# Distance attention: one add-and-maximum instruction per head and key tile in place of an add and a separate maximum per chunk

## The reference

```
q, k, v = ... .reshape(B, S, 16, 8)
scores = einsum('bqhd,bkhd->bhqk', q, k) / sqrt(8)
pos_emb = dist_emb[MAX_POS - 1 + distance]
scores = scores + einsum('bqhd,qkd->bhqk', q, pos_emb)
scores = scores + einsum('bkhd,qkd->bhqk', k, pos_emb)
probs = softmax(scores, axis=-1)
ctx = einsum('bhqk,bkhd->bqhd', probs, v)
```

## Time and profile before

| | us |
|---|---|
| median of 3 runs | 3696.86 |
| lowest and highest | 3695.2, 3696.99 |
| the profiled execution | 3662.5 |
| its span | 3660.7 |
| busy in the span: PE, DVE | 3164.8, 3031.9 |
| busy in the span: ACT, POOL | 2661.5, 996.2 |
| the distance attention in it | about 2230 to 3315 |

### The profile page before, as it was taken

The page is one execution under the profiler, slowest core; times in us unless marked ns, Lnnn a source line. Parts: engine busy times, 40 slices in busy tenths (PEclk is TensorE's granted clock), DMA queues, the critical chain, the costliest instruction groups (busy, mean ns, idle before and its releaser), DMA issues. The chain is left out here.

```text
span 3660.7 us, 70796 instructions
## 1 busy us (share of the span) xinstructions
PE 3164.8 (86%) x26908; PEld 2015.8 (55%) x26908; DVE 3031.9 (83%) x4286; ACT 2661.5 (73%) x2303; POOL 996.2 (27%) x1009
## 2 busy tenths in 40 slices
PE   4799999999999999999889756998999999998990
PEld 2233333333333333333568736888888888886890
DVE  8899999999999999999665576788788788786662
ACT  3799999999999999999444334776776776764430
POOL 2111111111111111111215355344343353330436
PEclk9899999999999999999879967999999999998995
DMA  5788898899888998898422254122122122102122
GB/s 157 293 334 338 338 341 332 341 342 342 333 339 338 341 341 332 340 345 337 179 76 56 60 192 77 30 41 41 29 38 43 28 37 43 28 11 76 46 62 68
DMA packets 311190, 683.32 MB, mean 187 GB/s; under 512 B 155281, under 2 KB 228466, under 8 KB 310418
## 3 DMA queue, kind: packets, MB, share of 16 engines
q1 hardware_dynamic: 302226, 661.80, 52.2%
q0 software_dynamic: 8704, 17.84, 2.1%
HBM read 90.66 MB, written 52.10 MB: 39 GB/s over the span
## 5 line engine op out<-in xcount | busy, mean ns | idle before, releaser
L1021 PE MATMUL psA<-wave,diag 128*128 128x512 f32 x2560 | 1171.2, 604 | 80.8 <-DVE score L1190 64.2
L1090 ACT ACTIVATE wave<-wave 128x2048 f32<-128x2048 int32 x640 | 1187.0, 1907 | 46.0 <-DMA wave<-score 39.5
L1021 PEld LDWEIGHTS psA<-wave,diag 128*128 128x128 f32 x2560 | 467.3, 190 | 687.9 <-issue 533.8
L953 POOL TENSOR_TENSOR diag<-ident,par 128x128 f32<-128x128 f32 x384 | 142.9, 401 | 1289.9 <-PE psA L1021 1289.4
L1143 DVE TENSOR_SCALAR score<-s,par 128x2048 int32<-128x2048 int32 x384 | 480.2, 1277 | 6.3 <-DMA wave<-score 6.1
L2248 POOL COPY kb<-ks 48x1024 bf16<-48x1024 bf16 x160 | 321.1, 2007 | 566.8 <-PE psR L2308 380.6
L1190 DVE SCALAR_TENSOR_TENSOR score<-wave,par,score 128x1024 f32<-128x1024 f32 x384 | 469.5, 1276 | 0.0
L1190 DVE SCALAR_TENSOR_TENSOR score<-wave,par,psA 128x1024 f32<-128x1024 f32 x256 | 315.6, 1273 | 47.7 <-PE psA L1021 47.4
L2398 ACT ACTIVATE W<-psR 128x1024 f32<-128x1024 f32 x256 | 249.5, 1023 | 133.3 <-PE psR L2333 133.2
L2389 ACT COPY r<-psR 128x1024 f32<-128x1024 f32 x256 | 248.6, 1020 | 102.4 <-PE psR L2308 102.4
L2435 DVE TENSOR_REDUCE mx<-S 128x8 f32<-128x1024 f32 x256 | 305.4, 1214 | 2.2
(11 more groups left out here) (287 smaller groups left out, 4795.1 us busy)
## 6 DMA issues: line engine op xcount, KB each, us to landing
wave<-score SPq DMA_DIRECT2D x384, 1023.9 KB, 6.3
wave<-s SPq DMA_DIRECT2D x128, 1023.9 KB, 4.8
ks<-kb_parts SPq DMA_DIRECT2D x56, 384.0 KB, 6.0
qs<-qb_parts SPq DMA_DIRECT2D x32, 384.0 KB, 6.3
ys<-f_ys SPq DMA_DIRECT2D x36, 256.0 KB, 2.5
wave_out<-og SPq DMA_DIRECT2D x33, 256.0 KB, 7.2
o<-wave_out SPq DMA_DIRECT2D x8, 1024.0 KB, 9.5
qp<-qa_parts SPq DMA_DIRECT2D x32, 192.0 KB, 7.1
```

Source lines behind the costliest of these rows:

```text
L1021: mm = pe.matmul(psA[:, kt, :], diag[:, h % 2, f, :], wave[:, h % 2, f, kt * L:(kt + 1) * L], start=(f == 0), stop=(f == PE_F - 1 or (h in ...
L1090: act.activation(wave[:, h % 2, f, :], angle[:, h % 2, f, :], ACT.Sin, scale=float(TWO_PI / 2.0 ** 32)).then_inc(sine, 1)
```

## The change

The add of a chunk, one instruction over 8 heads, becomes 8 instructions of one head each. Each adds the two parts, writes 128 columns of S, and leaves the maximum over them, taken with the lowest float32, in its place of `mx`. The last of the eight raises `dve_took`. The maximum steps of the first three units of a block and the semaphore `maxed` are gone; in the fourth unit the step keeps only the reduction from `mx` to `m`. The order on VectorE is otherwise as before, without the steps that are gone. TensorE, ScalarE, GpSimd and SyncE keep their instructions and order.

```diff
@@ -2034,6 +2034,7 @@
+    LOWEST = float(np.finfo(np.float32).min)
@@ -2081,13 +2082,12 @@
     def dve_head(u, q):
-        a, x = chunks("add", u), chunks("max", u)
+        a = chunks("add", u)
         ctx = [("ctx", q, 0)] if q is not None else []
-        return [a[0]] + ctx + [x[0], a[1], x[1], a[2], x[2], a[3], x[3]]
+        return [a[0]] + ctx + a[1:]
 
     def dve_mixed(u, ctx):
-        a, x = chunks("add", u), chunks("max", u)
-        return ctx + [a[0], a[1], x[0], x[1], a[2], a[3], x[2], x[3]]
+        return ctx + chunks("add", u)
@@ -2175,7 +2175,6 @@
-        maxed = sem(c, "maxed")
@@ -2425,17 +2424,18 @@
-                dve.tensor_tensor(part, psR[:, n % RING, :, :].rearrange("p a (h n) -> p (a h) n", n=P), second,
-                                  ALU.add).then_inc(dve_took, 1)
+                both = psR[:, n % RING, :, :].rearrange("p a (h n) -> p (a h) n", n=P)
+                for j in range(HB):
+                    h = k * HB + j
+                    ins = dve.tensor_tensor_reduce(out=part[:, j, :], in0=both[:, j, :], in1=second[:, j, :],
+                                                   scale=1.0, scalar=LOWEST, op0=ALU.add, op1=ALU.max,
+                                                   accum_out=mx[:, h, kt:kt + 1])
+                ins.then_inc(dve_took, 1)
 
             def maximum(u, k):
-                q, kt = u // QT, tile_of(u)
                 hs = slice(k * HB, (k + 1) * HB)
                 dve.wait_ge(dve_took, by_dve["c", u, k])
-                dve.tensor_reduce(mx[:, hs, kt], S[:, hs, kt * P:(kt + 1) * P], AX.X, ALU.max).then_inc(maxed, 1)
-                if u % QT == QT - 1:
-                    dve.wait_ge(maxed, 4 * u + k + 1)
-                    dve.tensor_reduce(m[:, hs], mx[:, hs, :], AX.X, ALU.max).then_inc(m_ready, 1)
+                dve.tensor_reduce(m[:, hs], mx[:, hs, :], AX.X, ALU.max).then_inc(m_ready, 1)
```

## The result

The changed kernel takes 3731.74 us, median of four runs (3731.34 to 3742.69), against 3696.93 for the kernel before: ratio 1.0097 over all runs (the two medians alone give 1.0094), 95% interval 1.0077 to 1.0117. It is slower, by 35 us. The direction was as forecast, and the time lies at the lower end of the range, but the forecast was +143 us, four times too much. Of the cases named, it came out near rival 1, for which 3730 had been worked out.

The account below looks back on a forecast made before the run. TensorE, nearly full, waits for PSUM slots that VectorE's adds free. Mixed units 5.56, first 2.05 and fourth 1.33 make 8.94 us a block, 143 over 16; with the median of 3696.86, forecast 3840 us, range 3725 to 4010.

Parts of the forecast that it names:

- rival 1: VectorE's additions: leaving the maximum is free, t = 0.20, +0.35 a mixed half, 3730 us in all; chance 0.15.
- What bounds the stage: Distance attention: TensorE nearly full, waiting for VectorE's adds to free PSUM slots; the maxima almost free, 0.10 us showing.
- One sign given for it: Waits in the distance attention: VectorE's wait for PE, 199.7 us before, was to become smaller.
- I take 0.27: VectorE's add-and-maximum: 0.27 us a step, the addition's 0.20 plus one more tiny instruction at 0.07.
- t: Time from one 128-column add's start to the next, 0.20 to 0.44 us; a slot is held for 8t and about 0.08.
- +2.05 and +1.33: Microseconds added per block in its first and its fourth unit, as later slots delay PE's chunks.
- the lower end: Lower limit of t: 0.20 us, the step of plain 128-column additions, if the maximum costs nothing.
- 33 and 143 us: Whole-stage losses over 16 blocks of queries: 33 us with t = 0.20, 143 us with t = 0.27.
- the copies would give some back: Where POOL's copies meet the subtractions, later subtractions could give back up to 8 us in four blocks.
- rival 3: TensorE idles in every half of the distance attention and its clock falls, windows under 0.9; chance 0.18.
- Rival 2: VectorE's instructions each wait for the one before or stream slower: t 0.33 to 0.44, 4167 us at 0.44; chance 0.20.
- Rival 4: Mixed halves: slot free earlier only under t = 0.155; at 0.134 a half gains 0.17, 3686 us; chance 0.02.

Follow-up runs that it names:

- E4: Changed kernel with the same instructions, each slot handed back to TensorE in halves: 3666.59 us, ratio 1.0028 to the kernel before.
- E3: Kernel before with wide adds but without its 256 maxima, the maximum left out of the softmax: 3648.54 us, ratio 0.9971.
- E1: Kernel before with each add cut into 8 plain additions, old separate maxima kept: 3712.77 against 3658.30 us, ratio 1.0148.
- E2: Changed kernel with plain additions that leave no maximum, the maximum left out of the softmax: 3685.30 us, ratio 1.0077 to the kernel before.
- E5: Changed kernel with slots handed over in halves both ways between TensorE and VectorE: 3692.35 us, ratio 0.9960 to the kernel before.
- E6: Kernel before with halves both ways, two adds of 512 columns and the old maxima: 3690.88 us, ratio 0.9956.
- E8: Halves both ways, wide adds and separate maxima in three units, new instruction only in the fourth: 3639.98 against 3658.24 us, ratio 0.9946.

## Why the prediction was right and wrong

- **What bounds the stage: right.** PE and VectorE meet in the slot; a longer hold is paid, the maxima were nearly free. E4 shows the first, E3 the second (10 us for 311), and E1 shows the loss without the new instruction. One sign given for it was wrong: VectorE's wait for PE was to be smaller, and it grew from 199.7 to 386.4 us, as its work had shrunk.
- **The step that failed is "I take 0.27".** The term was t, from one addition to the next: 0.20 to 0.44 by the rows, 0.27 chosen by charging one more small instruction in the queue, 0.07. No row of the kernel before shows an instruction of this kind, so the 0.27 was my estimate. The second instruction is there, but it starts when the next addition does, and costs 0.0085 a step against the earlier trace rows (0.211 for 0.2025), or 0.013 against the plain additions of E2 (0.198). At 16 steps in half a mixed unit, 0.06 too much each is 0.94 us a half. With the right t the first add and the second are spaced by PE again, not by VectorE, and of the +2.05 and +1.33 forecast for the first unit and the fourth, +0.78 and +0.14 are left.
- **The argument for the choice was the weak part.** Rows of small independent instructions were taken for the price of one that follows its own main instruction. The four small instructions of the earlier trace rows take a step of 0.07 (four in 0.36 us); the write of the maximum adds 0.0085 to 0.013. Its row differs in having no source (`mx<-`), but no run shows whether that is the reason. The row that lay nearest in kind was the addition alone, 0.20, the lower end.
- **The size of the error was foreseen, not its chance.** The text said that each 0.01 us of t costs 19 us. Below 0.27 its own sums, 33 and 143 us, make that 16. The choice of 0.07 over the lower end thus decided over 110 us, on one row of another operation. With such a slope the two ends are cases of like weight; 0.15 for the lower one looks too little now.
- **A small slip in the half.** With the maxima gone from the leg I set 2.01 for 2.11 and kept 1.69 for the next add, though that was 1.69 only because the first add had been 0.10 late. PE's own distance is 1.79 (before: position and content from 2395.38 to 2397.17), measured after as 1.80. So a half is 2.01 + 1.80 + 1.69 + 0.14 = 5.64, as measured; rival 1 had +0.35 a half where +0.56 came. It also means that the 0.10 of maxima was worth nothing in a mixed half: E3, without any, stays at 5.08. In return the stage grew by 41 us, where 16 blocks of +3.12 make 50: those in which GpSimd's copies fall on the subtractions, and the first one, lost less. That the copies would give some back the prediction had foreseen, up to 8 us. That rival 1's total was met to 2 us is therefore in part luck: its half was too short, and the blocks that lost less made up for some of that.
- **The clock (rival 3): this rival is out.** PE idled for some 11% of the two windows shown above, and the granted clock was 0.99 in both. The range had room for a clock that falls in most halves. No run shows such a fall (from 2500 to 3300 every run has 0.98 to 1.00 in each of its windows of 260 or 270 us), nor what it would cost a half.
- **Rival 2, a wait for the instruction before, is out:** it needed a step of 0.33, and it is 0.211.
- **Rival 4, faster, is out too,** for the reason given: the shortest step in the trace is 0.206. With 1.80 for 1.69 its threshold would have been 0.141 and not 0.155. E3 bounds it from the other side.

## What to carry to other kernels

Ask of a fused instruction not how much work it saves but what it does to the moment at which a shared buffer comes free: here the pass behind the release, 305.4 us of maxima, was worth 10 us (E3), and the one pulled ahead of it cost half a mixed unit what it added to the hold, 0.56 us a chunk, 0.45 of it for cutting the add and 0.11 for writing the maxima. Where an engine must hold a buffer longer, hand the buffer over in halves; here that took back 25 us of 35 with the same instructions, and beat the old kernel by 14 and 15 us when done in both directions (E5, E6). Where a forecast has a slope of 16 to 19 us for each hundredth of a microsecond in one unknown, the ends of that unknown are the cases, and the middle is only a guess.

## What the runs showed of the hardware

- An add-and-maximum of 128 columns out of PSUM is two records, 287 ns and 83 ns, and eight of them go at 0.211 us a step, where plain additions of the same size go at 0.2025 in the earlier trace rows and at 0.198 in E1 and E2. The second record starts with the next main instruction (0 ns between the two starts in all 1792 pairs inside a chunk of the profile after) and adds 0.013 us or less to the step. I had expected it to take its own step.
- Cutting one add of 1024 columns into 8 costs 0.45 us from the first start to the last end (1.67 in E1 and E2 against 1.22 before); leaving the maxima with them only 0.11 more (1.78).
- TensorE wrote one half of a slot, four heads, while VectorE read the other: in E5 the transpositions into the second half start at 2388.20 and the additions on the first at 2388.17, and their step stays 0.21, as it does in E4 and in the fourth unit of E8.
